# Spreading expert gates over the partitions: one turn into rows and a single 128-row product per expert and chunk

## The reference

```
logits = einsum('bld,ed->ble', x, gate_weight)      # 8 logits for each token
kth    = sort(logits.reshape(-1))[expert_k - 1]     # one threshold over all logits
gates  = logits * (logits >= kth)
h      = gelu(einsum('bld,ehd->bleh', x, w1) + b1)  # hidden width 1024 for each expert
y      = einsum('bleh,edh->blde', h, w2) + b2
out    = einsum('blde,ble->bld', y, gates)          # each expert's output times the token's gate
```

## Time and profile before

| | |
|---|---|
| three runs | 1154.92, 1159.92, 1160.14 us |
| median | 1159.92 us |
| the profiled execution | 1155.12 us, its span 1153.3 us |
| mean granted clock of TensorE | 0.933 of full speed |
| busy: PE, DVE, ACT, POOL | 1008.2, 687.2, 492.6, 258.0 us |
| the expert stage | from about 639 us to the end |

### The profile page before, as it was taken

One profiled execution on the slowest core, in us unless ns is written; L12 is line 12 of the kernel. 1 busy time (PEld: TensorE's weight loads), 2 busy tenths in 40 slices (PEclk: granted clock), 3 DMA queues, 4 the chain that ended last, 5 costly groups with the idle time before them and its releaser, 6 DMA issues.

```text
span 1153.3 us, 19123 instructions
## 1 busy us (share of the span) xinstructions
PE 1008.2 (87%) x7378; PEld 929.6 (81%) x7378; DVE 687.2 (60%) x1421; ACT 492.6 (43%) x1368; POOL 258.0 (22%) x215
## 2 busy tenths in 40 slices
PE   5779999987887498989898769899999999999998
PEld 5668887876566387878786769899999999999998
DVE  4764344443999835343644578775857575757653
ACT  3446364552865425645454322243333333333231
POOL 0232121241021111121215030161414141413111
PEclk9889999998677678999998879899999999999999
DMA  6120000011011010000002020110202020200001
GB/s 240 73 74 1 1 2 1 2 38 37 0 37 38 5 70 1 1 1 1 1 1 74 1 73 2 37 38 1 74 1 74 1 74 1 74 1 1 1 1 43
DMA packets 8638, 34.50 MB, mean 30 GB/s; under 512 B 610, under 2 KB 5090, under 8 KB 5220
## 3 DMA queue, kind: packets, MB, share of 16 engines
q1 hardware_dynamic: 8548, 33.28, 8.1%
HBM read 32.06 MB, written 1.22 MB: 29 GB/s over the span
## 4 chain that ended last, share of the span: by engine, by line
issue 32%; PE 31%; DVE 20%; POOL 9%; ACT 6%; DMA 1%; POOLq 0%; SPq 0%; DVEq 0%; ACTq 0%
PE D L458 15%; POOL wslot L404 5%; PE S L458 4%; ACT probs L866 4%; PE O L458 3%; PE O L612 3%; POOL h L301 3%; DVE probsT L1130 2%; PE T L596 2%; PE T L504 1%; DVE hid L1139 1%; DVE xc L1067 1%; DVE negmax L1113 1%; PE T L494 1%; DVE hid L1221 1%
## 5 line engine op out<-in xcount | busy, mean ns | idle before, releaser
L458 PE MATMUL O<-hid,wslot 128*128 128x300 f32 (+3 forms) x1728 | 256.4, 308 | 24.2 <-DVE rt L1229 14.1
L458 PEld LDWEIGHTS O<-hid,wslot 128*128 128x128 f32 x1728 | 247.8, 195 | 26.9 <-issue 14.4
L458 PE MATMUL D<-xn,wslot 128*128 128x300 f32 (+3 forms) x1248 | 211.7, 318 | 7.0 <-ACT work L991 6.2
L1322 DVE CAST hid<-work 128x300 fp32r<-128x300 f32 (+1 forms) x256 | 127.5, 498 | 135.3 <-ACT work L991 134.6
L458 PE MATMUL S<-xn,wslot 128*128 128x300 f32 (+3 forms) x1248 | 203.9, 312 | 0.0
L458 PEld LDWEIGHTS D<-xn,wslot 128*128 128x128 f32 x1248 | 188.9, 197 | 13.7 <-ACT work L991 6.4
L458 PEld LDWEIGHTS S<-xn,wslot 128*128 128x128 f32 x1248 | 186.0, 195 | 3.2 <-issue 2.5
L991 ACT ACTIVATE work<-D,prm 128x300 f32<-128x300 f32 (+1 forms) x128 | 64.2, 509 | 258.4 <-PE D L458 254.6
L1324 DVE TENSOR_TENSOR hid<-work,hid 128x300 fp32r<-128x300 f32 (+1 forms) x256 | 159.2, 622 | 8.8
L422 POOL TENSOR_TENSOR probs<-probs,rsum 111x444 f32<-111x444 f32 (+1 forms) x88 | 79.7, 905 | 300.7 <-DVE rsum L1122 300.7
L404 POOL TENSOR_TENSOR wslot<-raw,wslot 128x2048 fp32r<-128x2048 f32 x19 | 88.2, 4658 | 229.7 <-ACT wslot L808 229.7
(11 more groups left out here) (143 smaller groups left out, 1215.8 us busy)
## 6 DMA issues: line engine op xcount, KB each, us to landing
raw<-in_moe SPq DMA_DIRECT2D x16, 1024.0 KB, 4.8
raw<-in_attn SPq DMA_DIRECT2D x8, 1024.0 KB, 4.8
raw<-in_ffn SPq DMA_DIRECT2D x2, 1024.0 KB, 4.8
work<-in_x SPq DMA_DIRECT2D x2, 1008.0 KB, 9.5
raw<-in_x SPq DMA_DIRECT2D x1, 1008.0 KB, 7.7
out<-h SPq DMA_DIRECT2D x3, 300.0 KB, 2.8
raw<-in_w_lin SPq DMA_DIRECT2D x1, 768.0 KB, 4.4
vbuf<-in_x SPq DMA_DIRECT2D x1, 558.0 KB, 10.9
```

The source lines that it names most:

```text
L458: mm = pe.matmul(psum, a, b, start=(first and k == 0), stop=(k == 3 * n - 1))
L1322: nc.vector.tensor_copy(high, moe_g(s)[:, 0:w]).then_inc(m_high, 1)
```

## The change

The gates are turned once: `turn_gates(b)` makes, for each group of tokens, two products with the 8 gate columns as the stationary operand and the identity as the moving one, which puts the gates as rows on partitions 0 to 7 and, again, 64 to 71 of bank T0 or T1; 22 products in three batches. `keep_gates(b)` (DVE) stores the rows as fp32r in `gateT`, the high part in rows 0 to 7 and the low part in rows 64 to 71. `pick` has a one in rows e and 64+e of column e. One fp32r product of 300 columns with that column, broadcast to 128, then gives the gates of one expert and one chunk on all partitions (`spread_gate`). These 32 products stand singly behind up blocks: for experts 2 to 7 behind blocks 1, 3, 5 and 7 of chunk 1, and for experts 1 and 0 behind all eight blocks of step 6, which is (1, 2). ACT's copies stand behind the gelu of the same block. `moe_out` no longer waits for POOL in steps where nothing of the buffer ring is in use.

```
-            def spread_gates(e):
-                for c, (a, w) in enumerate(MCHUNKS):
-                    j = e * NC + c
-                    if j >= 2:
-                        pe.wait_ge(gb_act, j - 1)
-                    for g in range(a // GW, (a + w - 1) // GW + 1):
...
-                        mm = pe.matmul(BT[j % 2][:, lo - a:hi - a],
-                                       gates[0:nt, g * E + e:g * E + e + 1].to_broadcast([nt, P]),
-                                       ident[0:nt, lo - g * GW:hi - g * GW], start=True, stop=True)
-                    mm.then_inc(gb_mm, 1)
+            def turn_gates(b):
+                if b >= 2:
+                    pe.wait_ge(gt_ready, b - 1)
+                for k, g in enumerate(GT_BATCH[b]):
+                    for row in (0, DH):
+                        mm = pe.matmul(BT[b % 2][row:row + E, k * GW:k * GW + TM],
+                                       gates[0:TM, g * E:(g + 1) * E], ident[0:TM, 0:TM], ...)
+                mm.then_inc(gt_mm, 1)
+            def spread_gate(i):
+                e, c = SPREAD[i]
+                a, w = MCHUNKS[c]
+                if i == 0:
+                    pe.wait_ge(gt_ready, len(GT_BATCH))
+                    pe.wait_ge(gt_pick, 2)
+                if i >= 2:
+                    pe.wait_ge(gb_act, i - 1)
+                pe.matmul(BT[i % 2][:, 0:w], pick[:, e:e + 1].to_broadcast([P, P]), gateT[:, a:a + w],
+                          start=True, stop=True).then_inc(gb_mm, 1)
+        GT_BATCH = [range(k, min(k + 4, NG)) for k in range(0, NG, 4)]
+        SPREAD = [(e, c) for e in [1, 0] + list(range(2, E)) for c in range(NC)]
+        PLACE = {ec: i for i, ec in enumerate(SPREAD)}
+        def spread_at(e, c, m):
+            if e == 1 and c == 2:
+                return m
+            return PLACE[e, m // 2] if e >= 2 and c == 1 and m % 2 else None
...  moe_down (PE)
+                    if j == NC and dc == 0:
+                        turn_gates(2)
...  the steps of PE
                 if n == NC + 1:
                     pe.wait_ge(gates_ready, 1)
-                    spread_gates(0)
-                if c == 1 and e >= 1:
-                    spread_gates(e)
+                    pe.wait_ge(gt_zero, 1)
+                    turn_gates(0)
+                    turn_gates(1)
...  ACT, behind the gelu of a block
-                if c == 1 and m == KH - 1 and e >= 1:
-                    if e == 1:
-                        spread(0)
-                    spread(e)
+                if spread_at(e, c, m) is not None:
+                    spread(spread_at(e, c, m))
...  moe_first (POOL)
-            pool.wait_ge(gb_act, c + 1)
+            pool.wait_ge(gb_act, PLACE[0, c] + 1)
...  DVE
+            def keep_gates(b):
+                dve.wait_ge(gt_mm, b + 1)
...
+                for row in (0, DH):
+                    rows = slice(row, row + E)
+                    nc.vector.tensor_copy(tokens(gateT, rows, a), tokens(BT[b % 2], rows, 0)).then_inc(gt_high, 1)
+                dve.wait_ge(gt_high, 2 * b + 2)
+                low = tokens(gateT, slice(DH, DH + E), a)
+                nc.vector.tensor_tensor(low, tokens(BT[b % 2], slice(DH, DH + E), 0), low.bitcast(F32),
+                                        ALU.subtract).then_inc(gt_ready, 1)
...  moe_out1 (DVE)
-                dve.wait_ge(gb_act, e * NC + c + 1)
-                dve.wait_ge(h_moe, max(j - 3, 1))
+                dve.wait_ge(gb_act, PLACE[e, c] + 1)
+                if j >= KD * NC + 4:
+                    dve.wait_ge(h_moe, j - 3)
...  the steps of DVE
+                if n == NC + 1 and m == KH - 1:
+                    for b in range(len(GT_BATCH)):
+                        keep_gates(b)
```

More of the change, by code:

```diff
@@ L41 @@
 MCHUNKS = [(c * MW, min(MW, T - c * MW)) for c in range(NC)]
+TM = GI * TOK
 GROUPS = [list(range(c * GC, min((c + 1) * GC, NG))) for c in range(NC)]
@@ L98, in vit_tower @@
         addT = sb("addT", [P, KD, TOK])
+        gateT = sb("gateT", [P, NG * GW], F32R)
         b1r = sb("b1r", [BL + 1, FF], F32R)
@@ L101, in vit_tower @@
         b2u = sb("b2u", [P, KD])
+        pick = sb("pick", [P, E], F32R)
         gateR = sb("gateR", [P, 2, KD * E], F32R)
@@ L197, in vit_tower @@
         gates_ready = sem("gates_ready")
+        gt_zero = sem("gt_zero")
+        gt_pick = sem("gt_pick")
+        gt_mm = sem("gt_mm")
+        gt_high = sem("gt_high")
+        gt_ready = sem("gt_ready")
         gb_mm = sem("gb_mm")
@@ L968, in _, with spread @@
             square(3, 3)
-            def spread(e):
-                for c, (a, w) in enumerate(MCHUNKS):
-                    j = e * NC + c
-                    act.wait_ge(gb_mm, j + 1)
-                    if e >= 2:
-                        act.wait_ge(m_y, KD * ((e - 2) * NC + c + 1))
-                    nc.scalar.activation(moe_gate(e, c)[:, 0:w], BT[j % 2][:, 0:w], ACT.Copy).then_inc(gb_act, 1)
+            def spread(i):
+                e, c = SPREAD[i]
+                w = MCHUNKS[c][1]
+                act.wait_ge(gb_mm, i + 1)
+                if e >= 2:
+                    act.wait_ge(m_y, KD * ((e - 2) * NC + c + 1))
+                nc.scalar.activation(moe_gate(e, c)[:, 0:w], BT[i % 2][:, 0:w], ACT.Copy).then_inc(gb_act, 1)
             for s in range(E * NC * KH):
@@ L1020, in _ @@
             nc.vector.tensor_copy(gateR[:, 0, :], prm[:, S_GATE:S_END]).then_inc(params, 1)
+            nc.vector.memset(pick[:, :].bitcast(F32), 0.0).then_inc(gt_pick, 1)
             dve.wait_ge(params, 4)
@@ L1084, in prepare @@
                 dve.wait_ge(mats_in, 64)
+                dve.wait_ge(gt_pick, 1)
+                for row in (0, DH):
+                    ins = nc.vector.tensor_copy(pick[row:row + E, :], ident[row:row + E, row:row + E])
+                ins.then_inc(gt_pick, 1)
                 nc.vector.tensor_copy(masku[:, :], maskf[:, 2, :]).then_inc(masks, 1)
@@ L1260, in _ @@
             dve.wait_ge(o_mm[1], len(PAIRS))
+            nc.vector.memset(gateT[:, :].bitcast(F32), 0.0).then_inc(gt_zero, 1)
+            dve.wait_ge(gt_zero, 1)
             for t, value in ((logits, BIG), (keys, BIG), (gates, 0.0)):
@@ L1312, in gate, with tokens @@
                                                ALU.is_ge, ALU.mult).then_inc(gates_ready, 1)
+            def keep_gates(b):
+                dve.wait_ge(gt_mm, b + 1)
+                n, a = len(GT_BATCH[b]), GT_BATCH[b][0] * GW
+                def tokens(t, rows, a):
+                    return t[rows, a:a + n * GW].rearrange("p (g n) -> p g n", n=GW)[:, :, 0:TM]
+                for row in (0, DH):
+                    rows = slice(row, row + E)
[4 more added lines that the diff above has]
+                                        ALU.subtract).then_inc(gt_ready, 1)
             def moe_split(s):
```

8 lines of the change are left out of this document (5 added, 3 removed).

## The result

| | before | after |
|---|---|---|
| median of 7 runs | 1159.92 us | 1163.84 us |
| lowest to highest | 1154.92 to 1160.95 us | 1162.12 to 1167.63 us |
| ratio to before | | 1.0046, 95% interval 1.0026 to 1.0065 |
| the profiled execution, its span | 1155.12, 1153.3 us | 1166.95, 1165.2 us |
| mean granted clock | 0.933 | 0.924 |

The change costs 3.9 us by the medians and 5.3 us by the ratio (1159.92 x 0.0046). The forecast of 1175 us was +15 us. The time lies in the stated range; the size is wrong. The two profiled executions differ by 11.9 us of span. So part of the difference is not typical of the change, and the reading has to say which.

What follows compares the result with a forecast made beforehand. A chain from POOL's additions through its low parts and DVE's splits to `moe_out` bounds experts 2 to 6. +1.3 us at constant clock and +18 for clock falls make +19.3: 1174.4 or 1179 by base, set at 1175, range 1157 to 1186.

Steps and rivals of the forecast that it cites:

- The bound: Experts 2 to 6: POOL's low parts hold DVE ahead of six splits and `moe_out`, so PE's 2.6 us saving is waited out.
- wait in (e,2): Experts 2 to 6, chunk 2: PE idles 2.6 us ahead of `moe_down`, where it idled 0.96.
- wait in (e,1): Experts 2 to 6, chunk 1: PE idles 1.2 us ahead of `moe_down`, waiting for `moe_out`.
- expert 7: Last expert, no weights to prepare, DVE not held: the spread falls from 3.05 to 0.56 us, gain 2.5 us.
- step 7's wait: PE waits 2.3 us ahead of `moe_down`, as the later `moe_first` on POOL slows DVE's splits.
- steps 5 to 7 at constant clock: Turn of the gates to step 7's `moe_down`: +2.1 us, with bounds 0 and +4.
- rival 2: Experts 2 to 7: POOL's chain does not hold, PE's saving comes through, -7.4 us, 1152 us; chance 0.13.
- Rivals 3 and 4: ACT's copies between gelus hold PE, +13 us, chance 0.05; a spread product takes 0.28 us, not 0.14, 2 us, chance 0.03.
- The sum at a constant clock: Whole kernel without clock falls: 1.4 (experts 2 to 6) - 2.5 (expert 7) + 2.1 (steps 5 to 7) + 0.3 (start) = +1.3 us.
- The clock term: Step 5 to expert 6: PE's longer pauses drop its clock to 1.2 GHz, 18 us lost, from 0 to 23.
- The signs that were to show it right: Steps (2,2) to (6,2): clock at 0.50 for about 6.6 us behind most pauses, `moe_down` there taking nearly 10 us.
- rival 1: Expert stage: the clock stays full despite the pauses, 1156 to 1164 us, no measurable change; chance 0.17.

Runs made afterwards that it cites:

- moved low parts: POOL's two low parts for experts 3 to 7 moved behind the splits of (e,2) and (e,3): 1153.1 us on the kernel before, 1147.47 us on the changed kernel.
- cheap products: Kernel before, with the 14 fp32 gate products of each of experts 2 to 7 replaced by four fp32r products on other data: 1157.78 us, ratio 0.9996.

## Why the prediction was right or wrong

**The bound: right.** The chain from POOL's additions over its low parts and two DVE instructions to `moe_out` ends the wait in (e,2), with PE's saving waited out. The moved low parts and the cheap products show it, and the profile after has the numbers ("at constant clock" is without the loss by falls of the clock):

| step of the prediction | predicted | measured |
|---|---|---|
| wait in (e,1) | 1.2 us | 1.03 |
| wait in (e,2) | 2.6 us | 2.38 |
| an expert at full clock | +0.28 us | +0.29 (58.67 against 58.38) |
| expert 7 | -2.5 us | -2.4 |
| 32 records of the turn | 1.8 us | 1.62 |
| pause between the halves of `moe_down(1,0)` | 3.7 us | 3.73 |
| step 7's wait | 2.3 us | 2.96 |
| steps 5 to 7 at constant clock | +2.1 us | 2.6 |

The order of POOL's first low part and DVE's cast stayed as it was (828.54 and 828.84), so rival 2 did not come. Rivals 3 and 4 neither: ACT's copies did not hold the blocks, and a product took 0.14 us. The sum at a constant clock was predicted at +1.3 us. Measured is 1.4 (five experts, the 4.6 less two falls) + 2.6 (steps 5 to 7, the 4.2 less one) - 2.4 = +1.6. What the start added (0.3 predicted) can't be read: the pause at 650 us ends between 649.2 and 651.9 in the nine profiles with the changed start and between 650.0 and 651.8 in the four with before's, and behind it 3.1 us hang on the low clock of the threshold scores.

**The clock term: wrong in size.** This is the step that failed: "I count 4 of 5 experts at 3.2 us = 12.8, the pause of 3.7 at 3.0 (a part of the low stretch is still idle), and 0.7 of one for the 2.3: 2.2. Together 18 us". Measured: three falls at 1.5 to 1.6 us, 4.7 in the profile. Both factors were too large, each about twofold. The signs that were to show it right say the same: low stretches "of about 6.6 us" were 3.4 long, behind two of the five pauses, and a `moe_down` of "nearly 10 us" took 8.2.
- The cost. I took the 6.6 us of the earlier trace rows for a time in which PE is busy. Before 735.60 PE was idle (the pause of 5.10 ended there), and the clock had fallen some 3 us earlier. So about half of that low stretch cost nothing. In the expert stage a pause of 2.4 us is over when the clock falls, and then only 3.4 us are low: 1.54 us by 8.22 against 6.68. That is not so everywhere. In before's second attention, behind the pause of 2.21 us that ended at 447.06, the clock was low for 6.8 us with PE mostly busy:
```profile
449.20:455.80 6.60, 6.18 (x42) 5.09 (x43) 3.11 (x8) 5.05 (x29) 2.83 (x4) 0.50 0.02 4
```
So the 6.6 us were a true reading of before, and carrying them over to another stretch was the error; why the low stretch is shorter there is not shown. A price of up to 2.8 exists in the expert stage too, behind pauses of more than 3.3 us, of which the change makes none but the 3.73, and even that one cost 1.6 (4.95 us for a half of `moe_down`, 773.80-768.85, against 3.35).
- The count. Five pauses of before, all followed by a fall, were taken as a rule for the new ones. They stand in the attention and early up blocks, in a less dense stream. In the expert stage 2 of 5 lost the clock, and 11 of 25 over the study. The forecast saw the difference ("a pause of 2.6 us may be forgiven after it") and gave it 0.17, as all or nothing.

With 0.4 falls for each of six pauses and one sure, at 1.55 us, the term is 5.3 us. With the +1.3 it gives 6.6, against 3.9 to 5.3 measured. These two numbers were fitted afterwards, in part on the same profile, so the agreement proves nothing. A small misreading besides: one of before's five falls came 2.3 us behind the end of its pause (341.02 to 343.3), not within 2.1.

The Trainium skill (TensorE: Matmul & The Clock Gate, section on why this matters for your kernels) advises against pauses of over about 3 us between bursts. The prediction made that a sum of about 4 us, close to the measured. The trace does not bear the rule out as it stands: here the clock also fell behind pauses of 1.82 to 2.71 us, in 11 of 25 cases, and two of after's three falls stand behind such pauses. So that sum comes near by leaving out part of the falls and pricing the one it counts too high.

**The base.** The sum was +19.3 us, 1174.4 on the profiled execution and 1179 on the median. The 1175 put down is only +15.1 on the median, so that mixing the two bases took 4.2 us off an error of the clock term. That is luck and no merit of the mechanism. The runs of one kernel are up to 6 us apart.

**The chances.** Slower by over 0.5% had 0.67 and same 0.19; the measured 0.3 to 0.5% lies at the border. The direction was right, and the 0.62 on 1168 to 1184 was misplaced. The measured 1163.84 is inside 1157 to 1186 only because the lower end was set by rival 1; it is within rival 1's own 1156 to 1164, though the clock did not stay.

## What to carry to other kernels

When an engine that looks full gets work taken away, follow the next wait of it over one more step: here PE's 2.6 us were returned in full until a slow POOL instruction was moved into DVE's idle time, and then the same edit was worth 6 us. Move the long GpSimd instruction first, shorten PE afterwards. And price a fall of the clock by the busy time that lies in the low stretch, not by the stretch, and take both its length and how often it comes from the same stretch of the kernel, not from another.

## What the runs showed of the hardware

- Pauses of PE of the same length do not always do the same: of pauses of 2.38 us in one execution two lost the clock and three did not. In the expert stage all 11 of 3.3 us and more did. What decides between them was not found.
- Low stretches in the expert stage last 3.4 or 6.8 us, in the threshold scores 6.8 or 13.7, there with PE busy all the time (13.00 of 13 us at 0.50 in after), and without a pause ahead of the fall (3.20 of 3.2 us at 1.00, from 656.6 on).
- POOL's low part holds DVE to one instruction for its whole length, 4.70 us for a cast that takes 0.30 alone, and 4.76 for a subtraction. The Trainium skill (SBUF — State Buffer, who interferes with whom) speaks of an exclusive lock on the shared port pair; the trace agrees. Beside POOL's shorter instructions of 0.8 to 1.2 us a split took 1.8 us instead of 0.8.
